# Two recurrent layers on one core: set-up and routing joined into one stage, the two best experts found by successive maxima, gated scan results kept in the gate's buffer

## What is computed

```python
# layer 0, scan part (after a layer norm of x), state N = 16
z = sigmoid(x @ Wz + bz);  x_ssm = x @ Wx + bx
Bm, C = x @ WB + bB, x @ WC + bC;  dt = softplus(x @ Wdt + bdt)
h_t = exp(dt * -exp(A_log)) * h_(t-1) + x_ssm * dt * Bm      # 512 steps, per batch
y = (sum over N of h_t * C) * z;  out = y @ Wout + bout
# layer 0, experts: 8 experts, each token goes to its 2 most probable
probs = softmax(x @ router_w.T);  token_probs, idx = top_k(probs, 2)
out = sum over the 2 of p * ((gelu(x @ wg.T + bg) * (x @ w1.T + b1)) @ w2.T + b2)
```

## Time and profile before

| | us |
|---|---|
| median of 3 runs (lowest, highest) | 1458.49 (1452.99, 1463.76) |
| the profiled execution | 1462.59 |
| its span, from first to last instruction | 1460.8 |
| set-up, until SP's first request for rows of x | 33.28 |
| routing, until DVE's last instruction of it | 106.74 |
| experts, until POOL's first gather of layer 1 | 413.20 |

### The profile page before, as it was taken

The page is one execution under the profiler, slowest core; times in us unless marked ns, Lnnn a source line. Parts: engine busy times, 40 slices in busy tenths (PEclk is TensorE's granted clock), DMA queues, the critical chain, the costliest instruction groups (busy, mean ns, idle before and its releaser), DMA issues.

```text
span 1460.8 us, 21614 instructions
## 1 busy us (share of the span) xinstructions
PE 1207.0 (83%) x7497; PEld 735.5 (50%) x7497; DVE 995.2 (68%) x1661; ACT 687.9 (47%) x1324; POOL 273.8 (19%) x332
## 2 busy tenths in 40 slices
PE   2637969969935888999988999999999999998944
PEld 2527858858922433444543454455455455454333
DVE  2886767767936677697598789688778777544223
ACT  0335836737622353444654653664563544443421
POOL 0006424424230310220120041031032201000000
PEclk9967989989966767998999998998998999898877
DMA  3809867858725214224324423433433411210101
GB/s 71 257 1 305 271 203 246 282 187 265 228 91 115 93 61 109 77 94 95 104 75 103 115 92 91 102 112 88 118 100 90 97 44 30 39 45 17 38 23 36
DMA packets 99525, 168.38 MB, mean 115 GB/s; under 512 B 25972, under 2 KB 53468, under 8 KB 99356
## 3 DMA queue, kind: packets, MB, share of 16 engines
q1 hardware_dynamic: 76636, 90.98, 23.3%
q0 software_dynamic: 22784, 76.04, 16.6%
HBM read 142.68 MB, written 11.17 MB: 105 GB/s over the span
## 4 chain that ended last, share of the span: by engine, by line
PE 45%; DVE 9%; ACT 6%; DMA 6%; issue 4%; SPq 1%; POOL 1%; POOLq 0%; DVEq 0%; ACTq 0%
PE bank L1166 10%; PE bank L1184 4%; PE bank L1201 4%; PE bank L1265 3%; PE bank L1169 3%; PE bank L1361 3%; PE bank L1204 3%; PE bank L1231 3%; PE bank L1235 2%; DMA q_all<-turned_rows 2%; ACT probs L1376 2%; DMA rec_wide<-head_recips 2%; PE bank L1222 2%; DVE sc_state L382 1%; PE bank L1353 1%
## 5 line engine op out<-in xcount | busy, mean ns | idle before, releaser
L1531 DVE TENSOR_REDUCE neg_max<-bank 128x2 f32<-128x1024 f32 (+3 forms) x256 | 203.9, 817 | 168.8 <-PE bank L1204 158.5
L1376 ACT ACTIVATE probs<-bank 128x1024 f32<-128x1024 f32 (+1 forms) x192 | 169.1, 881 | 285.4 <-PE bank L1169 274.3
L1166 PE MATMUL bank<-q_all,kk 49*128 49x512 f32 (+3 forms) x1024 | 223.7, 515 | 37.9 <-ACT probs L1376 26.3
L309 POOL DMA_DIRECT2D sc_bc_wide<-scan_bc x128 | 73.1, 571 | 507.4 <-DVE sc_ub L375 262.0
L735 PE MATMUL bank<-xcol,wst 128*128 128x128 f32 x1152 | 150.5, 287 | 1.7 <-DMA wst<-bias_cols 1.6
L382 DVE TENSOR_TENSOR_SCAN sc_state<-sc_a,sc_ub 128x1024 f32<-128x1024 f32 x64 | 145.9, 2279 | 0.1
L735 PEld LDWEIGHTS bank<-xcol,wst 128*128 128x128 f32 x1152 | 144.4, 204 | 2.4 <-DMA wst<-bias_cols 2.4
L1166 PEld LDWEIGHTS bank<-q_all,kk 49*128 49x128 f32 x1024 | 81.2, 194 | 116.3 <-ACT probs L1376 47.6
L852 POOL DMA_INDIRECT xrow<-sorted_in,token_of x72 | 87.6, 1216 | 258.9 <-PE bank L726 141.6
L1201 PE MATMUL bank<-kr,q_all 48*128 48x512 f32 (+3 forms) x512 | 113.1, 438 | 21.2 <-DVE neg_max L1531 13.9
L875 DVE SCALAR_TENSOR_TENSOR hid<-bank,wst,gel 128x128 f32<-128x128 f32 x288 | 80.3, 340 | 65.9 <-issue 45.4
(11 more groups left out here) (273 smaller groups left out, 1880.2 us busy)
## 6 DMA issues: line engine op xcount, KB each, us to landing
sc_bc_wide<-scan_bc POOLq DMA_DIRECT2D x128, 512.0 KB
wst<-in_wexp SPq DMA_DIRECT2D x72, 512.0 KB
q_all<-q_kind SPq DMA_DIRECT2D x96, 128.0 KB, 4.3
rec_wide<-head_recips SPq DMA_DIRECT2D x32, 256.0 KB
p_t<-gates_turned SPq DMA_DIRECT2D x16, 512.0 KB
sorted_out<-xrow SPq DMA_DIRECT2D x8, 576.0 KB
rows_all<-in_x SPq DMA_DIRECT2D x8, 256.0 KB, 4.9
w<-in_wexp SPq DMA_DIRECT2D x1, 2048.0 KB, 9.7
```

Of the source, the lines that this page charges most:

```text
L1166: mm(bank[1][:, par, at:at + n], kk[rows, b % 2, kt * P:(kt + 1) * P], q_all[rows, quad // 2 % 3, pair, kt * P:L].bitcast(F32), start=True ...
L1376: af(probs[:, slot % RING, :, 0:width], bank[1][:, :, 0:width], ACT.Exp, scale=0.125).then_inc(s["p_ready"], 1)
L1531: last = v.tensor_reduce(neg_max[:, quad % 2, i, pr:4:2], bank[0][:, :, at:at + (i + 1) * P], AX, ALU.max, negate=True)
```

## The change

- The set-up stage is gone as a stage: its loads, matmuls, copies and casts move into `route`, and the barrier between them is gone. SP asks for batch 0 of x first, then for the identity and the router, the other seven batches, and then the rest in four groups, each with its own semaphore.
- What DVE cast and cleared goes to POOL, what it copied from PSUM to ACT. PE runs the latents behind the projections dt and bc of batch 0 and ahead of the counts, the values behind the projection z.
- The ranks are replaced: the greatest probability, the first expert that has it (`firsts`), that one lowered by 2, and the same again. All operations are over 128x256 elements; one of 128x512 and one reduction of it replace two pairs when slots are looked up.
- `gate` writes into z's buffer and `project_out` reads it there; `weigh` waits for the gate (`sc_yz`), `take_z` for the projection (`sc_outp`).
- In the experts' loop `SCAN_TILE` is -1, so batches 1 and 2 start at tiles 23 and 47. x is projected at tiles 19 and 43 as before, but ACT copies it to SBUF (`take_x`) and PE waits for that alone; DVE multiplies two tiles later (`multiply_u`). The gated result is projected out at tiles 27 and 51, z at tiles 29 and 53, and these are `late` tiles.

```diff
-SETUP_IN = len(WEIGHTS) - len(LATE) - len(DRAM_ONLY) + 2
+FIRST = ("ident", "router0")
+COUNTS = ("before", "ones", "steps", "tiles")
+SCAN_PARTS = ("wdt", "wbc", "bdt", "bbc", "wx", "wz", "bx", "bz", "a_log", "wout", "bout")
+OTHERS = ("wq_nope_t", "wkvb_t", "wo_nope", "mask", "mask_t", "wq", "wk", "lower")
...
-            nc.all_engine_barrier()
         route(nc, sems_of_stage, bk, c, x, xs, locals())
         experts0(nc, sems_of_stage, bk, c, xs, ys, locals())
...
     def project_out(self, pe, b, to):
-            last = self.nc.tensor.matmul(to[:, j * P:(j + 1) * P], self.v["y"][:, 0, j * P:(j + 1) * P], self.c["wout"][:],
+            last = self.nc.tensor.matmul(to[:, j * P:(j + 1) * P], self.v["z"][:, j * P:(j + 1) * P], self.c["wout"][:],
...
     def take_z(self, act, b, at):
         act.wait_ge(self.s["sc_zp"], b + 1)
         if b >= 1:
-            act.wait_ge(self.s["sc_yz"], b)
+            act.wait_ge(self.s["sc_outp"], b)
...
+    def take_x(self, act, b, at):
+
+        act.wait_ge(self.s["sc_xp"], b + 1)
+        if b >= 2:
+            act.wait_ge(self.s["sc_u"], b)
+        self.nc.scalar.activation(self.v["xn_t"][:], at, ACT.Identity, bias=self.c["bx"][:]).then_inc(self.s["sc_x"], 1)
+
+    def multiply_u(self, dve, b):
+        s, v = self.s, self.v
+        dve.wait_ge(s["sc_x"], b)
+        dve.wait_ge(s["sc_dt"], b + 1)
+        self.nc.vector.tensor_tensor(v["u"][:], v["xn_t"][:], v["dt"][:], ALU.mult).then_inc(s["sc_u"], 1)
...
         if k == 0 and b >= 1:
-            dve.wait_ge(s["sc_outp"], b)
+            dve.wait_ge(s["sc_yz"], b)
...
-        self.nc.vector.scalar_tensor_tensor(v["y"][:, 0, :], v["z"][:], 1.0, v["y"][:, 1, :], ALU.add, ALU.mult).then_inc(s["sc_yz"], 1)
+        self.nc.vector.scalar_tensor_tensor(v["z"][:], v["z"][:], 1.0, v["y"][:, 1, :], ALU.add, ALU.mult).then_inc(s["sc_yz"], 1)
...
                 for b in range(B):
                     sp.dma_start(rows_all[:, b * J:(b + 1) * J, :], x_v[b]).then_inc(x_landed[b], 16)
+                    if b == 0:
+                        for name in FIRST:
+                            load(name, s["first_in"])
+                for name in COUNTS:
+                    load(name, s["counts_in"])
+                for name in SCAN_PARTS:
+                    load(name, s["scan_in"])
...
+                for name in OTHERS:
+                    load(name, s["others_in"])
...
+                        load(name, t["late_in"])
...
+                sp.dma_start(t["w2"][:, :].rearrange("p (e f) -> p e f", e=E),
+                             w["wexp"].rearrange("p (e f) -> p e f", e=E)[:, :, 2 * FF:]).then_inc(t["late_in"], 16)
...
+                sp.wait_ge(s["biases_split"], 5)
+                for part in range(3):
+                    sp.dma_start(t["bias16"][part:part + 1, :], bias_part[:, part, :]).then_inc(s["rows16_in"], 16)
...
+                             t["bcol"][:, :].rearrange("p (e k) -> p e k", e=E)[:, :, 0:2 * FT]).then_inc(s["rows16_in"], 16)
...
-                mm(bk(5)[:, 0:P], c["ones"][:], c["before"][:], start=True, stop=True)
-                mm(bk(5)[:, P:P + 1], c["before"][:], c["ones"][:, 0:1], start=True, stop=True).then_inc(s["counted_psum"], 1)
+                pe.wait_ge(s["first_in"], 16 * len(FIRST))
...
+                pe.wait_ge(s["scan_in"], 16 * len(SCAN_PARTS))
                 scan.project("dt", bk(6), xn_t_all[:, 0:L])
                 scan.project("bc", bk(7), xn_t_all[:, 0:L])
+                pe.wait_ge(s["counts_in"], 16 * len(COUNTS))
+                mm(bk(5)[:, 0:P], c["ones"][:], c["before"][:], start=True, stop=True)
+                mm(bk(5)[:, P:P + 1], c["before"][:], c["ones"][:, 0:1], start=True, stop=True).then_inc(s["counted_psum"], 1)
...
+                nc.tensor.transpose(bk(3)[:, 0:E * XB // P], bias_rows[:, :],
+                                    c["ident"][0:E * XB // P, 0:E * XB // P]).then_inc(s["cols_psum"], 1)
+                pe.wait_ge(s["others_in"], 16 * len(OTHERS))
+                for h in range(H):
...
+                last.then_inc(s["latent_psum"], 1)
                 pe.wait_ge(s["picked_ready"], 1)
...
                 scan.project("x", bk(6), xn_t_all[:, 0:L])
                 scan.project("z", bk(7), xn_t_all[:, 0:L])
+                for h in range(H):
...
                 act.wait_ge(s["shifted"], 1)
                 af(prob[:], prob[:], ACT.Exp).then_inc(s["exp_ready"], 1)
+                act.wait_ge(s["scan_in"], 16 * len(SCAN_PARTS))
+                af(neg_a[:], c["a_log"][:], ACT.Exp).then_inc(s["decay_ready"], 1)
                 scan.take_bc(act, 0, bk(7))
                 scan.take_dt(act, 0, bk(6))
+                act.wait_ge(s["counted_psum"], 1)
+                af(counted[:], bk(5)[:, 0:P], ACT.Copy).then_inc(s["counted_ready"], 1)
+                af(lane[:], bk(5)[:, P:P + 1], ACT.Copy).then_inc(s["lane_ready"], 1)
                 scan.logarithm(act, 0)
...
+                    for par in range(2):
+                        last = af(wq_kind[:, 2, tile, 64 * par:64 * par + 64].rearrange("p (f pp) -> p pp f", pp=4),
+                                  latent[:, tile, par, :, :], ACT.Copy)
...
                 scan.take_z(act, 0, bk(7))
...
+                for n in range(4):
+                    last = af(wvo[32 * n:32 * n + LAT, :, :], bk(2)[32 * n:32 * n + LAT, :].rearrange("p (g f) -> p g f", g=4), ACT.Copy)
...
+            @block.gpsimd
+            def _(pool):
+                link = chain_of(pool, s["pool_chain"])
+                g_ = nc.gpsimd
+                g_.memset(eps[:], EPS).then_inc(s["eps_ready"], 1)
...
+                split = chain_of(pool, s["biases_split"])
+                split(g_.tensor_copy(bias_part[:, 0, :], b2[:]))
...
+                pool.wait_ge(s["others_in"], 16 * len(OTHERS))
+                pool.wait_ge(s["first_in"], 16 * len(FIRST))
+                g_.tensor_copy(t["ident16"][:], c["ident"][:])
...
+                dve.wait_ge(s["counts_in"], 16 * len(COUNTS))
+                link(v.tensor_scalar(order[:], c["tiles"][:, 0:E], -1.0, float(E), ALU.mult, ALU.add))
                 dve.wait_ge(s["logits_ready"], 1)
-                link(v.tensor_copy(prob[:], bk(4)[:, 0:T * E].rearrange("p (j e) -> p j e", j=T)))
...
+                link(v.tensor_reduce(small[:, :, 0:1], logits, AX, ALU.max))
+                v.tensor_tensor(prob[:], logits, of_row(0), ALU.subtract).then_inc(s["shifted"], 1)
...
                 for k in range(2):
-
-                    link(v.scalar_tensor_tensor(chosen[:], rank[:], float(k), prob[:], ALU.is_equal, ALU.mult))
-                    link(v.tensor_reduce(t["gate2"][:, k, 0:T].unsqueeze(2), chosen[:], AX, ALU.add))
-                v.tensor_scalar(picked[:], rank[:], 1.5, None, ALU.is_lt).then_inc(s["picked_ready"], 1)
+                    best = t["gate2"][:, k, 0:T].unsqueeze(2)
+                    link(v.tensor_reduce(best, among[:], AX, ALU.max))
+                    link(v.tensor_tensor(firsts[:, k, :, :], among[:], best.to_broadcast([P, T, E]), ALU.is_ge))
+                    link(v.tensor_tensor(firsts[:, k, :, :], firsts[:, k, :, :], order[:].unsqueeze(1).to_broadcast([P, T, E]), ALU.mult))
+                    link(v.tensor_reduce(small[:, :, 3:4], firsts[:, k, :, :], AX, ALU.max))
+                    link(v.tensor_tensor(firsts[:, k, :, :], firsts[:, k, :, :], of_row(3), ALU.is_equal))
+                    if k == 0:
+                        link(v.scalar_tensor_tensor(left[:], firsts[:, 0, :, :], -2.0, prob[:], ALU.mult, ALU.add))
+                        among = left
+                v.tensor_tensor(picked[:], firsts[:, 0, :, :], firsts[:, 1, :, :], ALU.add).then_inc(s["picked_ready"], 1)
...
-                for k in range(2):
-                    link(v.scalar_tensor_tensor(chosen[:], rank[:], float(k), slot[:], ALU.is_equal, ALU.mult))
-                    link(v.tensor_reduce(slot_f[:, k, :].unsqueeze(2), chosen[:], AX, ALU.add))
+                link(v.tensor_tensor(chosen[:], firsts[:], slot[:].unsqueeze(1).to_broadcast([P, 2, T, E]), ALU.mult))
+                link(v.tensor_reduce(slot_f[:].unsqueeze(3), chosen[:], AX, ALU.add))
...
-                link(v.memset(t["scan"]["a"][:, :, :, 0:1], 0.0))
...
-SCAN_TILE, TILES_A_CHUNK = -3, 3
+SCAN_TILE, TILES_A_CHUNK = -1, 3
...
-                    if (b := scan_due(m + 2)) is not None and b >= 1:
+                    if (b := scan_due(m + 4)) is not None and b >= 1:
...
                         scan.project("x", beside, xn_t_all[:, b * L:(b + 1) * L])
-                    if (b := scan_due(m - 2)) is not None and b >= 1:
+                    if (b := scan_due(m - 4)) is not None and b >= 1:
                         pe.wait_ge(s["xcol_ready"], m + 2)
...
-                    if (b := scan_due(m - 3)) is not None and b >= 1:
+                    if (b := scan_due(m - 6)) is not None and b >= 1:
...
-                        pe.wait_ge(scan.s["sc_u"], b + 1)
```

(14 more changed lines are left out.)

237 lines of the change are left out of this document (104 added, 133 removed).

## The result

The changed kernel took 1390.51 us (median of 4 runs, 1385.23 to 1395.94), the kernel before 1461.12 beside it; the ratio is 0.952 with a 95% interval of 0.946 to 0.958. The profiled execution has a span of 1390.7 us against 1460.8. The forecast was 1391.

The account below looks back on a forecast made before the run. It saw early holes as one routing chain led by rows and DVE, and the experts' stage as PE waiting at batch take-overs. Routing 37.8, experts 30.1 and layer 1's 1 sum to 68.9 off 1462.6; forecast 1391 us, range 1383 to 1400.

Parts of the forecast that it names:

- Rows first: Set-up: asking for batch 0's rows at 0.74 instead of 33.28 us gains 32.2 us, second batch late by some 0.3.
- Two best: Routing: shorter expert search on DVE, partly given to the latents on PE, gains 5.1 us; 3.5 more at 2.4 GHz.
- Slots: Routing: one pair of DVE operations instead of two, and the memset gone, gains 0.5 us.
- Start of the experts: Experts' stage: first hid no longer stands behind the scan's step and weigh on DVE, gaining 3.5 us.
- Take-overs: Experts' stage, batch to batch: three PE waits go, 33.2 us gained, less 4.0 for z and 2.0 for DVE's extra work.
- End: End of the experts' stage: last add and gate stand beside PE's last down instead of ahead of two tiles, gaining 2.4 us.
- Transfers: Experts' stage: the same bytes in less time fit with little to spare, so 3.0 us is taken off the gain.
- Layer 1: Layer 1: weigh no longer waits for L293, 0.82 us in each of two places, of which 1 us is counted.
- Rivals: 1 and 5: Experts: transfers or DVE replace the waits, 1402 to 1414, chance 0.15; PE stays at lower clock, up to 1590, chance 0.01.
- Rival 3: Experts' stage: batch take-over only moved, late tile with z or finish costs what sc_u did; about 1418, chance 0.05.
- rival 4: More gained: latents at 2.4 GHz (3.5), transfers and DVE costing nothing (5); 1382, chance 0.09.
- Rival 2: Set-up: POOL's 22 small operations hold up DVE's normalising, losing 5 to 10 us; 1396 to 1401, chance 0.08.

Follow-up runs that it names:

- finish_first: Changed kernel with DVE's finish placed ahead of hid, instead of behind it, in the tiles taking the scan's result; ratio 0.946 to before, experts' stage 272.50 us.
- tile_m2: Changed kernel with the scan starting one tile earlier in every batch (SCAN_TILE -2 instead of -1); one run, experts' stage 281.85 us.
- mid: Changed kernel with finish ahead of hid and PE's five scan operations moved between the two halves of up; ratio 0.948 to before.
- z_off_late: Changed kernel with z's projection and activation one tile later (tiles 30 and 54 instead of 29 and 53); ratio 0.953 to before.
- few_rows: Changed kernel with the experts' row loads writing 16 partitions instead of 128 from the third chunk on; one run, experts' stage 275.83 us.

## Why the prediction was right

The time was met because misses of both signs cancel: +2.9 in routing, -3.2 with the experts, +1.6 in layer 1. That the total came within 2 us is luck; that most of each part was had is not.

- *Rows first*: 32.2 forecast, the logits moved 31.7. DVE's first statistics came at 3.51 (3.6 forecast); the second batch was late, by 0.7 instead of 0.3. Right.
- *Two best*: mis-sized. The search took 8.2 us behind the logits, as said. The term was 5.1, by the latents at 7.0 us; it measured 8.5, since they ran at 2.4 GHz. The prediction had this as its other end (3.5 more), with the right mechanism and the wrong choice: 8 of 11 executions have it so. finish_first is the forecast's own case, counts 11.8 behind the logits where 12.2 was said.
- *Slots*: 0.5 forecast, 0.4 measured.
- *Start of the experts*: 3.5 forecast, 5.1 measured. tile_m2 shows that the place of the first scan is the cause. PE's wait for the first `hid` fell from 4.8 to 1.0 us; the other 1.3 I have not traced.
- *Take-overs*: 27.2 net forecast, 21.2 measured. The step that failed is the count of the three waits as gone. Those for `sc_u` and the gate are; that for `sc_rows` is not (5.0 of 6.7 left, where "no wait of more than 2 us" was said). I asked whether the gate was ready and not where `finish` stands in DVE's queue, and had charged DVE's extra work 1.0 each when it comes back through this wait. finish_first and mid show DVE's backlog as its cause; in the first take-over the clock's fall adds 1.5. The 4.0 for z were too much: PE does wait for z's activation where it did not before, but 1.2 each time, 2.5 and not 4.0, and the late tile is not the cause (z_off_late): ACT's rows have z behind the decays, which no run moved. Against the 3.0 charged to each take-over the rows have 6.8 in the first (4.3 for `sc_rows` with the clock, 1.2 for z, 1.3 of smaller waits for `hid`, `wst` and `xrow`) and 5.8 in the second (2.3, 1.2 and 2.3). Taken from 16.6 that leaves 9.8 and 10.8, where 9.7 and 11.5 were measured.
- *End*: 2.4 forecast (its terms add up to 2.6), a loss of 1.1 measured, within a scatter of 2 us. The sum moved the add and the gate and left out that the scan's other operations move with them; the rows show PE waiting for DVE's last `hid` and for the gate. That this is the cause is not shown: moving the scan back by one tile did not shorten the end.
- *Transfers*: 3.0 forecast, 2 to 5 by the waits that few_rows removes. One sign that the prediction named for being wrong did show, if weakly: PE's waits for `wst` rose from 1.6 us to 4.6.
- *Layer 1*: 2.6 measured, 1 forecast, inside the scatter of 1042 to 1058. Not shown either way.
- *Rivals*: 1 and 5 did not come; the granted clock of the stage rose from 0.92 to 0.97. Rival 3 (priced at 26, where the sum's own terms give 27.2) came in small: `finish` still holds PE up for 5.0 us in two waits, where `sc_u` did for 13.5. Half of rival 4 came, the latents. Rival 2 was held improbable, and is true as a rule: it stayed away only by the size and place of POOL's operations.

## What to carry to other kernels

When a wait is removed, ask of each result that is taken at that place who takes it, and what stands in that engine's queue; an engine that did its extra work while the other waited now does it late. A term that hangs on TensorE's clock level has two prices: take it off the path where that is free, and quote both where it is not. Operations given to GpSimd are free beside VectorE only next to some of its operations, so look at which they meet.

## What the hardware showed that I had not expected

- PE ran the same 32 small matmuls in 4.1 to 4.8 us in 8 executions and in 7.00 in 3, after the same work without a gap. Its clock first rose 6.5 to 8.0 us behind the start of the last logits in the 8, and 18.9 to 19.8 in the 3.
- After waits of PE of 2.2 to 2.7 us at the take-overs the next 16 matmuls took 2.7 to 3.3 us instead of 1.96 nine times out of 17; after the seven waits of 0.5 to 1.7 us there they took 1.96 every time.
- VectorE's TENSOR_SCALAR on 128x128 was held by GpSimd's work (four in 4.09 instead of 1.11 us), its BATCH_NORM_STATS2 was not (0.86).
- The transfers reached 372 GB/s over 38 to 45 us, above the 358 that the trace of before had as its peak and that the prediction named as a limit. The Trainium skill ("Perfetto Trace Analysis", Roofline) says that one active core can pull more than 358; the trace agrees.
